# Feed-forward steps in another order: both score pairs around gate and up, the moments, then twelve down products, with a third bank for the scores

## The chip, the core and the metric

The kernel runs on one core of a Trainium2 chip. The metric is the device time of one execution in microseconds (us); the time before is the median of three runs. The engines are TensorE (PE in the profile, its weight loads PEld), VectorE (DVE), ScalarE (ACT), GpSimd (POOL) and SyncE (SP, which here only issues DMAs). They run their own instruction queues in order and meet at semaphores. TensorE writes to eight PSUM banks of 512 float32 columns.

## The reference

Eight batches of 256 rows by 512 columns go through two blocks:

```python
x = x + _L0_attn_ref(_L0_cond_ref(x, cond_2048[:, None, :], L0_cond_b), ...)   # causal conv, attention of 16 heads of 32
x = x + _L0_ffn_ref(_L0_cond2_ref(x, cond_2048, Wq, Wk, Wv, b), gate_cp, up_cp, down_cp)
...
gate = jnp.einsum('bsh,ih->bsi', hidden_states, gate_w)   # ih: 2048 x 512, from cubic splines of control points
up = jnp.einsum('bsh,ih->bsi', hidden_states, up_w)
inter = jax.nn.silu(gate) * up
return jnp.einsum('bsi,hi->bsh', inter, down_w)
```

The second attention (`cond2`) has 16 heads of 16 over 512 positions with a masked softmax; its result feeds the feed-forward network.

## The kernel before

The work is a software pipeline over batches. In the loop over batches 1 to 6 (and in batch 7 written out behind it) the second attention of batch b runs together with the feed-forward network of batch b - 1. Batch 0 has no feed-forward part, and the one of batch 7 runs alone at the end (the tail). GpSimd computes the convolution of batch b + 1 meanwhile: two operations, then seven pairs of a product (line 562) and an add (line 565), each on two SBUF operands, for every batch but the last.

**The window.** The change lies in the loop `for n in range(NT + 1)` of `batch` on TensorE, nine steps n = 0 to 8, each with the n-th 256 rows of the inner dimension 2048. In a step stand:
- `gate_up(b, n + 1)`, four products (eight records) on tiles of 64 rows, in banks 3 and 4. ScalarE takes the silu (line 604), VectorE multiplies (`gated`, line 780), ScalarE rounds the product to a high part (`inter_rounded`, line 611), and VectorE makes the low part (`rest`, line 785, two SBUF operands).
- `moments(b, n + 3)`, eight products (sixteen records) on tiles of 32 columns, from the attention result `y` and a table; ScalarE copies them to `z` (line 594), which gate and up of step n + 2 read.
- two pairs of `scores` from step 1 on (line 1131, 52 rows each, one of a pair on the upper and one on the lower half of the array), 32 in the window. Each is one bank; VectorE takes its row maximum (`maximum`, line 863).
- `down(b, n - 1, 1)` and `down(b, n, 0)`, six full-size products each (lines 995 to 997), into banks 6 and 7. The weights come in three slots by `load_weights` on SyncE, each when `down_step` says that a slot is free.

Step 5 (`TURN_STEP`) has `turn(0)`, a transpose of the first 16 maxima, from which `max_rows` makes rows for `shifted`. Steps 5 to 7 have no moments, steps 7 and 8 no gate and up; in step 8 `shifted(0)` and `shifted(1)` write banks 2 to 5.

**What sets the order.** Everything is written out by hand, on each engine, with counting semaphores. VectorE's loop over the same n has two maxima, `gated(n + 1)`, the turn in step 5, two maxima, `rest(n + 1)`. ScalarE's `feed` has per step `silu(n + 1)`, the copy of the moments, `inter_rounded(n + 1)`. The last one waits for TensorE as well, because `inter_h` has two slots; `down_step` counts the calls `down(b, m, 1)`:

```python
act.wait_ge(S["inter_out"], fed(b, "inter_out", n + 1))
if n >= 2:
    act.wait_ge(S["down_step"], fed(b, "down_step", n - 1))
nc.scalar.activation(r(inter_h[:, n % 2]), inter[:, n % 2], ACT.Copy).then_inc(S["inter_high"], 1)
```

A score waits until the maximum of the last score in its bank is taken: `wait("s2_max", last_in_bank + 1)`. The first score waits for `stack2_0` as well, twelve copies by SyncE (`stacks2(0)`, line 420) into `q2` and `k2`. Behind the window follow sixteen rounds with `shifted`, the other scores and `values2`.

Of the kernel before, what the change touches and what calls it, by code (L numbers as in the profile page):

```python
# [7 lines left out]
ACT = mybir.ActivationFunctionType  # L8
# [8 lines left out]
B, L, D = 8, 256, 512  # L17
# [14 lines left out]
NT = IT // 2  # L32
ZR = 32
# [29 lines left out]
WINDOW_SCORES = 4 * (NT + 1 - WINDOW_FROM)  # L63


AHEAD = 2
TURN_STEP = WINDOW_FROM + GS // 4
# [7 lines left out]
OUT_AT = tuple(CT * (g + 1) + (1 if CT * (g + 1) + 1 not in TURN_AT or g else 2) for g in range(NG - 1))  # L75


SCORE_BANKS = [s % 2 for s in range(WINDOW_SCORES)]
for _k in range(1, 1 + (NS - WINDOW_SCORES) // 4):
    for _s in range(4):  # L80
        _free = (0, 1) if _k in TURN_AT or _k in OUT_AT else (7, 0, 1)
        SCORE_BANKS.append(min(_free, key=lambda x: len(SCORE_BANKS) - 1 - SCORE_BANKS[::-1].index(x)
                               if x in SCORE_BANKS else -1))


FIRST_BANKS = [(0, 1, 3, 4)[s % 4] if s < WINDOW_SCORES - 4 else SCORE_BANKS[s] for s in range(NS)]
# [11 lines left out]
Q2_BANKS = (2, 5)  # L98
K2_BANKS = (6, 7)
V2_BANKS = (0, 1, 2, 5)  # L100
Z_BANKS = (2, 5)
GU_BANK, SUM_BANK = 3, 6
TURN_BANKS = (Z_BANKS[0], 7, 7, 7)

# [44 lines left out]
def fed(b, name, count):  # L149

    return b * PER_FEED[name] + (count - PER_FEED[name])


def block_program(nc, x_lanes, x_rows, taps, conv_b, qkv_wT, qk_b, v_b, out_wT, out_b, slopes, cond, w2T, att_b,
# [7 lines left out]
    with ExitStack() as ctx:  # L162
# [6 lines left out]
        psum = ctx.enter_context(nc.psum_tensor("psum", [P, 8, 512], F32))  # L169
# [51 lines left out]
        zt = sb("z_table", [P, CT, NT * 2 * ZR])  # L221
# [351 lines left out]
        def _(act):  # L573
# [16 lines left out]
            def z_copy(b, n):  # L590
                act.wait_ge(S["z_ready"], fed(b, "z_ready", n + 1))
                if n >= 2:
                    act.wait_ge(S["gu_ready"], fed(b, "gu_ready", n - 1))
                nc.scalar.activation(z[:, n % 2, :], psum[:, Z_BANKS[n % 2], 0:L], ACT.Copy).then_inc(S["z_out"], 1)

            def moments_out(b):
                for n in range(AHEAD):
# [138 lines left out]
        def _(dve):  # L736
# [64 lines left out]
            def batch(b, first=False, last=False):  # L801
# [88 lines left out]
                for n in range(NT + 1):  # L890
                    for s in window_pair(n, 0):
                        maximum(s)
                    if not first and n + 1 < NT:
                        gated(b, n + 1)
                    if n == TURN_STEP:
                        turn(0)
                    for s in window_pair(n, 1):
                        maximum(s)
                    if not first and n + 1 < NT:
                        rest(b, n + 1)  # L900
                if not first:
# [48 lines left out]
        def _(pe):  # L950
# [14 lines left out]

            def moments(b, n):
                if n >= 2:
                    pe.wait_ge(S["z_out"], fed(b, "z_out", n - 1))
                for i in range(2):
                    for s in range(4):  # L970
                        c = 2 * (s % 2) + i
                        cols = slice((2 * (n % NT) + s // 2) * ZR, (2 * (n % NT) + s // 2 + 1) * ZR)
                        last = nc.tensor.matmul(psum[s * ZR:(s + 1) * ZR, Z_BANKS[n % 2], 0:L], zt[:, c, cols],  # L973
                                                y[:, c, :], start=i == 0, stop=i == 1, skip_group_check=True)
                last.then_inc(S["z_ready"], 1)

# [59 lines left out]
            def batch(b, first=False, last_batch=False):  # L1036
                def wait(name, count):
                    pe.wait_ge(S[name], at(b, name, count))
# [74 lines left out]
                def scores(s):  # L1113
                    banks = FIRST_BANKS if first else SCORE_BANKS
                    last_in_bank = (FIRST_LAST_IN_BANK if first else LAST_IN_BANK)[s]
                    g, n = s // GS, s % GS
                    if n == 0:
                        wait(f"stack2_{g}", 192)
                        if g == 0:
                            wait("aug_rows", 64)  # L1120
                    if s < len(set(banks[:WINDOW_SCORES])):
                        wait("v2_out", CT)
                    elif last_in_bank is None:
                        wait("max2_low", 2)
                    else:
                        wait("s2_max", last_in_bank + 1)
                    if banks[s] == 7 and s >= WINDOW_SCORES + 4 * (OUT_AT[0] - 1):
                        wait("y_out", 1)
                    e, i, t = n % 2, n // (2 * CT), n // 2 % CT
                    rows = slice(e * ROWS2, e * ROWS2 + MAX2)  # L1130
                    nc.tensor.matmul(psum[:, banks[s], :], r(q2[rows, g, i, t * P:(t + 1) * P]),  # L1131
                                     r(k2[rows, g, i, :]), start=True, stop=True).then_inc(S["s2_ready"], 1)

                def turn(g):
                    wait("s2_max", GH * CT * (g + 1))
                    if g == 0 and first:
                        wait("v2_out", CT)
                    elif g == 0:
                        pe.wait_ge(S["z_out"], fed(b, "z_out", NT - 1))
                    elif g < NG - 1:  # L1140
                        wait("max2_low", g)
                        if g == 1 and first:
                            wait("k2_out", LT)
                        elif g == 1:
                            pe.wait_ge(S["sum_out"], fed(b, "sum_out", LT))
                    else:
                        wait("y_out", 1)
                    nc.tensor.transpose(psum[0:GH * CT, TURN_BANKS[g], 0:P], max2[:, g].rearrange("p e h t -> p (e h t)"), ident[:])\
                        .then_inc(S["max2_turned"], 1)

                def shifted(j):
                    g, u = j // (2 * CT), j % (2 * CT)
                    if u == 0:
                        wait("max2_rows", 64 * (g + 1))
                    if j < 2:
                        wait("v2_out", CT)
                        wait("k2_out", LT)
                        wait("max2_low", 1)
                        if first:
                            wait("s2_max", WINDOW_SCORES - 4)  # L1160
                        else:
                            pe.wait_ge(S["inter_out"], fed(b, "inter_out", NT))
                    else:
                        wait("p2_out", j - 1)
                    kt = u // 2
                    for e in range(2):
                        rows = slice(e * ROWS2, e * ROWS2 + END2)
                        last = nc.tensor.matmul(psum[:, 2 + u % 2 * 2 + e, :], r(k2[rows, g, u % 2, kt * P:(kt + 1) * P]),  # L1168
                                                r(q2[rows, g, u % 2, :]), start=True, stop=True)
                    last.then_inc(S["t2_ready"], 1)  # L1170
# [26 lines left out]
                    pe.wait_ge(fixed2, 64)  # L1197
                else:
                    wait("k2_out", LT)
                for n in range(NT + 1):  # L1200
                    if not first and n + 1 < NT:
                        gate_up(b, n + 1)
                    if not first and n == 0:
                        wait("v2_out", CT)
                        moments(b, AHEAD)
                    if not first and n + AHEAD + 1 < NT:
                        moments(b, n + AHEAD + 1)
                    for s in window_pair(n, 0):
                        scores(s)
                    if n == NT:  # L1210
                        shifted(0)
                    if n == TURN_STEP:
                        turn(0)
                    if not first and n:
                        down(b, n - 1, 1)
                    for s in window_pair(n, 1):
                        scores(s)
                    if n == NT:
                        shifted(1)
                    if not first and n < NT:  # L1220
                        down(b, n, 0)

                for k in range(1, ROUNDS + 1):
                    if k < ROUNDS:
# [226 lines left out]
```

## Time and profile before

| what | value |
|---|---|
| median of three runs | 1317.77 us |
| lowest and highest | 1312.59 and 1326.76 us |
| span of the profiled execution (no other time is recorded for it) | 1322.0 us |
| TensorE busy | 1216.3 us (92%) |
| VectorE busy | 780.9 us (59%) |
| ScalarE busy | 507.2 us (38%) |
| GpSimd busy | 355.0 us (27%) |
| maxima, line 863 | 512, 327.0 us busy |
| `rest`, line 785 | 64, 83.5 us busy, mean 1304 ns |

The busy shares are averages over the whole span. A window with its nine steps takes some 44 of the roughly 154 us of a batch. Where a line has the same operation at many places, the timeline of one stretch shows what it stands beside.

### The profile page before, as it was taken

What the parts mean: (1) busy time and instruction counts of PE and PEld (TensorE: products, weight loads), DVE (VectorE), ACT (ScalarE), POOL (GpSimd) and SP (SyncE); (2) the same over time, 40 slices, a digit from 0 to 9 for tenths busy, and PEclk for the clock granted to TensorE, in tenths of its full rate; (3) what the DMA queues carried; (4) which work ended last, traced back from release to release, by engine and by line L of the source; (5) the groups of instructions that cost most, each with busy time, mean ns of one, the idle gap of its engine ahead of it and who ended that gap; (6) DMA issues with size and microseconds to landing.
All of it is one profiled execution on the core that took longest, in us unless ns stands there. A gap on an engine that the chain in (4) does not pass through costs nothing.

```text
span 1322.0 us, 20809 instructions
## 1 busy us (share of the span) xinstructions
PE 1216.3 (92%) x7400; PEld 672.6 (51%) x7400; DVE 780.9 (59%) x1173; ACT 507.2 (38%) x699; POOL 355.0 (27%) x201
## 2 busy tenths in 40 slices
PE   5685789999999999999999999999999999999988
PEld 4352245554555545555546545555355555465436
DVE  7676644578445882568635783467725675356822
ACT  1131243334533265223633256322552336332572
POOL 3183770092003800075000910048000740000000
PEclk9687689998999999999999999999899989999999
DMA  8989604382226704265044822267042640448024
GB/s 294 279 318 309 175 2 112 139 193 103 49 67 173 238 23 112 98 154 182 14 102 146 208 80 66 53 178 229 23 112 108 167 159 15 100 149 221 36 113 175
DMA packets 81057, 180.89 MB, mean 137 GB/s; under 512 B 14468, under 2 KB 54356, under 8 KB 71284
## 3 DMA queue, kind: packets, MB, share of 16 engines
q1 hardware_dynamic: 70864, 161.56, 42.1%
q10 hardware_dynamic: 8832, 13.91, 3.1%
q0 software_dynamic: 1280, 4.20, 0.9%
q8 instruction: 68, 1.11, 0.4%
q14 instruction: 13, 0.11, 0.0%
HBM read 106.41 MB, written 21.14 MB: 96 GB/s over the span
## 4 chain that ended last, share of the span: by engine, by line
PE 75%; DVE 8%; DMA 6%; POOL 5%; issue 3%; ACT 2%; SPq 1%; ACTq 0%; DVEq 0%; POOLq 0%
PE psum L1181 9%; PE psum L1131 8%; PE psum L955 8%; PE psum L995 5%; PE psum L984 5%; PE psum L973 4%; PE psum L961 4%; DMA products<-in_gu_points 4%; DVE max L863 4%; PE psum L996 4%; PE psum L997 4%; PE psum L1089 4%; PE psum L1100 4%; PE psum L1168 3%; PE psum L1052 3%
## 5 line engine op out<-in xcount | busy, mean ns | idle before, releaser
L863 DVE TENSOR_REDUCE max<-psum 128x1 f32<-128x512 f32 x512 | 327.0, 684 | 111.3 <-PE psum L1131 109.4
L699 ACT ACTIVATE probs<-psum 128x1024 f32<-128x1024 f32 x256 | 248.0, 1022 | 168.2 <-PE psum L1168 166.9
L1131 PE MATMUL psum<-k,q 52*128 52x512 f32 x512 | 186.7, 514 | 28.8 <-DMA k<-low 15.2
L555 POOL TENSOR_TENSOR h<-h_in,tap 128x1024 f32<-128x1024 f32 x7 | 13.3, 1897 | 604.9 <-DVE low L766 604.9
L1131 PEld LDWEIGHTS psum<-k,q 52*128 52x128 f32 x512 | 79.3, 199 | 165.6 <-DVE max L863 129.5
L1181 PE MATMUL psum<-probs,v 128*32 128x512 f32 x1024 | 145.7, 643 | 0.4 <-ACT probs L699 0.3
L1168 PE MATMUL psum<-q,k 54*128 54x512 f32 x512 | 116.8, 452 | 14.7 <-DMA q<-max_l 7.2
L565 POOL TENSOR_TENSOR h<-h,products 128x1024 f32<-128x1024 f32 x49 | 123.5, 2520 | 3.8
L995 PE MATMUL psum<-stack 128*128 128x512 f32 x256 | 113.7, 444 | 0.0
L764 DVE CAST high<-low 128x1024 fp32r<-128x1024 f32 x32 | 25.3, 790 | 148.3 <-ACT low L586 120.6
L955 PE MATMUL psum<-h,qkv_w 128*128 128x256 f32 x448 | 105.9, 390 | 4.1 <-POOL h L565 4.1
L955 PEld LDWEIGHTS psum<-h,qkv_w 128*128 128x128 f32 x448 | 84.5, 194 | 32.7 <-issue 21.9
L996 PE MATMUL psum<-stack 128*128 128x512 f32 x256 | 100.9, 394 | 0.0
L997 PE MATMUL psum<-stack 128*128 128x512 f32 x256 | 100.3, 392 | 0.0
L785 DVE TENSOR_TENSOR stack<-probs,stack 128x512 fp32r<-128x512 f32 x64 | 83.5, 1304 | 26.7 <-ACT stack L611 26.7
L562 POOL TENSOR_TENSOR products<-h_in,tap 128x1024 f32<-128x1024 f32 x49 | 97.2, 1983 | 3.3
L653 ACT ACTIVATE probs<-psum 128x768 f32<-128x768 f32 x64 | 49.0, 810 | 92.9 <-PE psum L1072 92.9
L833 DVE RECIPROCAL inv<-psum 128x256 f32<-128x256 f32 x32 | 56.2, 1758 | 44.8 <-PE psum L1052 43.9
L611 ACT ACTIVATE stack<-probs 128x512 fp32r<-128x512 f32 x64 | 40.4, 631 | 109.5 <-DVE probs L780 102.5
L604 ACT ACTIVATE probs<-psum 128x512 f32<-128x512 f32 x64 | 38.2, 597 | 111.7 <-PE psum L984 111.7
L1168 PEld LDWEIGHTS psum<-q,k 54*128 54x128 f32 x512 | 55.3, 196 | 47.6 <-ACT probs L699 26.1
L961 PE MATMUL psum<-qkv_w,h 128*128 128x512 f32 x128 | 71.1, 677 | 2.7 <-issue 2.7
(112 smaller groups left out, 1645.7 us busy)
## 6 DMA issues: line engine op xcount, KB each, us to landing
stack<-wd_sorted SPq DMA_DIRECT2D x64, 1024.0 KB, 6.7
stack<-high SPq DMA_DIRECT2D x128, 128.0 KB, 2.4
stack<-low SPq DMA_DIRECT2D x64, 128.0 KB, 2.4
q<-high SPq DMA_DIRECT2D x128, 64.0 KB, 4.3
k<-high SPq DMA_DIRECT2D x128, 64.0 KB, 2.5
h_in<-in_x_lanes SPq DMA_DIRECT2D x9, 512.0 KB, 3.9
x<-in_x_rows SPq DMA_DIRECT2D x8, 512.0 KB, 7.9
x_scratch<-x SPq DMA_DIRECT2D x8, 512.0 KB, 3.9
```

Source lines behind the costliest of these rows:

```text
L562: nc.gpsimd.tensor_tensor(products[:], h_in[:, :, k:k + L], over(tap[:, :, k:k + 1]), ALU.mult)\
L565: nc.gpsimd.tensor_tensor(h[:], h[:], products[:], ALU.add).then_inc(S["conv_step"], 1)
L699: nc.scalar.activation(probs[:, u // 2 % 2, u % 2 * 2:u % 2 * 2 + 2, :], psum[:, 2 + u % 2 * 2:4 + u % 2 * 2, :], ACT.Exp)\
L863: nc.vector.reduce_max(max2[:, g, e, i, t:t + 1], psum[:, bank, :], AX_X).then_inc(S["s2_max"], 1)
L955: last = nc.tensor.matmul(psum[:, o % 2, 0:L], qkv_w[:, c, o * P:(o + 1) * P], h[:, c, :], start=c == 0, stop=c == CT - 1)
L961: last = nc.tensor.matmul(psum[:, V1_BANKS[t], :], h[:, c, t * P:(t + 1) * P], qkv_w[:, c, 2 * D:3 * D], start=c == 0, stop=c == CT - 1)
L995: nc.tensor.matmul(psum[:, SUM_BANK + s, :], r(inter_h[lhs]), r(w_h), start=n + g == 0, stop=False)
L996: nc.tensor.matmul(psum[:, SUM_BANK + s, :], r(inter_h[lhs]), r(w_l), start=False, stop=False)
L997: last = nc.tensor.matmul(psum[:, SUM_BANK + s, :], r(inter_l[lhs]), r(w_h), start=False, stop=n == NT - 1 and g == 1)
L1131: nc.tensor.matmul(psum[:, banks[s], :], r(q2[rows, g, i, t * P:(t + 1) * P]), r(k2[rows, g, i, :]), start=True, stop=True).then_inc(S["s2 ...
L1168: last = nc.tensor.matmul(psum[:, 2 + u % 2 * 2 + e, :], r(k2[rows, g, u % 2, kt * P:(kt + 1) * P]), r(q2[rows, g, u % 2, :]), start=True, ...
L1181: last = nc.tensor.matmul(psum[e * BLK:(e + 1) * BLK, 6, :], v2[:, t, head, :], probs[:, t % 2, e, :], start=t == 0, stop=t == CT - 1, ski ...
```

## The change

TensorE's step is written in another order: first score pair, gate and up, second score pair, in step 5 the turn, moments, `down(b, n - 1, 1)`, `down(b, n, 0)`. Step 8 stands behind the loop with its order as before. The scores of the window rotate over banks 0, 1 and 5 (the last four over 0 and 1) where they alternated between 0 and 1. Bank 5 is taken from the moments, which use bank 2 alone from the fifth on and so wait for the copy just before. VectorE takes the third maximum of a step ahead of `gated`, and the turn behind the fourth.

```diff
+def least_recent(banks, free):
+    return min(free, key=lambda x: len(banks) - 1 - banks[::-1].index(x) if x in banks else -1)
...
+    SCORE_BANKS.append(least_recent(SCORE_BANKS, (0, 1, 5) if _s < WINDOW_SCORES - 4 else (0, 1)))
...
-Z_BANKS = (2, 5)
+Z_BANKS = (2, 5, 2, 5, 2, 2, 2, 2)
...
                 for n in range(NT + 1):
                     for s in window_pair(n, 0):
                         maximum(s)
+                    for s in window_pair(n, 1)[:1]:
+                        maximum(s)
                     if not first and n + 1 < NT:
                         gated(b, n + 1)
+                    for s in window_pair(n, 1)[1:]:
+                        maximum(s)
                     if n == TURN_STEP:
                         turn(0)
-                    for s in window_pair(n, 1):
-                        maximum(s)
                     if not first and n + 1 < NT:
                         rest(b, n + 1)
...
-                    pe.wait_ge(S["z_out"], fed(b, "z_out", n - 1))
+                    pe.wait_ge(S["z_out"], fed(b, "z_out", n - 1 if n <= 2 * AHEAD else n))
...
+                        if banks[s] == Z_BANKS[1] and not first:
+                            pe.wait_ge(S["z_out"], fed(b, "z_out", 2 * AHEAD))
...
-                        if first:
-                            wait("s2_max", WINDOW_SCORES - 4)
-                        else:
+                        wait("s2_max", WINDOW_SCORES - 4)
+                        if not first:
                             pe.wait_ge(S["inter_out"], fed(b, "inter_out", NT))
...
-                for n in range(NT + 1):
+                for n in range(NT):
+                    for s in window_pair(n, 0):
+                        scores(s)
                     if not first and n + 1 < NT:
                         gate_up(b, n + 1)
+                    for s in window_pair(n, 1):
+                        scores(s)
+                    if n == TURN_STEP:
+                        turn(0)
...
                     if not first and n + AHEAD + 1 < NT:
                         moments(b, n + AHEAD + 1)
-                    for s in window_pair(n, 0):
-                        scores(s)
-                    if n == NT:
-                        shifted(0)
-                    if n == TURN_STEP:
-                        turn(0)
                     if not first and n:
                         down(b, n - 1, 1)
-                    for s in window_pair(n, 1):
-                        scores(s)
-                    if n == NT:
-                        shifted(1)
-                    if not first and n < NT:
+                    if not first:
                         down(b, n, 0)
```

TensorE, step 1 of a batch's window, before (line 984 gate and up, 973 moments, 1131 scores, 995 to 997 down):

```order
L984 MATMUL psum<-z,w_gate_up 128x256 x4
L973 MATMUL psum<-y,z_table 32x256 x8
L1038 ISA x2
L1131 MATMUL psum<-k,q 128x512 x2
L995 MATMUL psum<-stack 128x512
L996 MATMUL psum<-stack 128x512
```

The same place in the changed kernel (991 gate and up, 980 moments, 1140 scores, 1002 to 1004 down):

```order
L1140 MATMUL psum<-k,q 128x512 x2
L985 REGISTER_ALU
L991 MATMUL psum<-z,w_gate_up 128x256 x4
L1131 REGISTER_ALU
L1140 MATMUL psum<-k,q 128x512
L1045 REGISTER_ALU
L1140 MATMUL psum<-k,q 128x512
L980 MATMUL psum<-y,z_table 32x256 x8
L1002 MATMUL psum<-stack 128x512
L1003 MATMUL psum<-stack 128x512
```

All four scores stand ahead of the moments now, and all twelve down products behind them.

VectorE, one step of the window, before (863 maxima, 780 `gated`, 785 `rest`; in the changed kernel 868, 785 and 790):

```order
L863 TENSOR_REDUCE max<-psum 128x1
L803 REGISTER_ALU
L863 TENSOR_REDUCE max<-psum 128x1
L779 REGISTER_ALU
L780 TENSOR_TENSOR probs<-psum,probs 128x512
L803 REGISTER_ALU
L863 TENSOR_REDUCE max<-psum 128x1
L803 REGISTER_ALU
L863 TENSOR_REDUCE max<-psum 128x1
L785 TENSOR_TENSOR stack<-probs,stack 128x512
```

and in the changed kernel:

```order
L790 TENSOR_TENSOR stack<-probs,stack 128x512
L808 ISA
L868 TENSOR_REDUCE max<-psum 128x1
L808 REGISTER_ALU
L868 TENSOR_REDUCE max<-psum 128x1
L808 REGISTER_ALU
L868 TENSOR_REDUCE max<-psum 128x1
L784 REGISTER_ALU
L785 TENSOR_TENSOR probs<-psum,probs 128x512
L808 REGISTER_ALU
L868 TENSOR_REDUCE max<-psum 128x1
L790 TENSOR_TENSOR stack<-probs,stack 128x512
```

The third maximum has moved ahead of `gated`; `rest` is still the last of the step, and ahead of the next step's first maximum.

## Rows read from the trace of the kernel before

**Rows 1.** The page: the chain of waits that ended last, by engine.

```profile
PE 75%; DVE 8%; DMA 6%; POOL 5%; issue 3%; ACT 2%; SPq 1%; ACTq 0%; DVEq 0%; POOLq 0%
```

**Rows 2.** Stretches of core 0: us, busy time by engine, PEclk, DMA share, GB/s.

```profile
575.60:581.72 6.12, 6.12 (x41) 3.58 (x41) 4.53 (x7) 1.62 (x3) 5.88 (x4) 1.00 0.61 100
...
600.06:604.97 4.91, 4.91 (x26) 3.18 (x25) 3.91 (x9) 1.23 (x2) 4.75 (x3) 1.00 1.04 223
604.97:610.96 5.99, 5.46 (x25) 3.35 (x25) 5.99 (x8) 1.93 (x3) 2.19 (x1) 1.00 0.98 398
610.96:614.97 4.01, 4.01 (x17) 2.47 (x16) 2.91 (x5) 0.79 (x2) 2.37 (x2) 1.00 0.05 19
```

**Rows 3.** The timeline of TensorE, step 2: start us, us, engine, line, operation.

```profile
581.72 1.14 PE L984 MATMUL psum<-z,w_gate_up 64*128 64x256 f32 x8
...
582.78 1.07 PE L973 MATMUL psum<-y,z_table 128*32 128x256 f32 x16
...
583.78 0.50 PE L1131 MATMUL psum<-k,q 52*128 52x512 f32 x2
...
584.22 0.53 PE L995 MATMUL psum<-stack 128*128 128x512 f32 x1
...
585.28 0.40 PE L996 MATMUL psum<-stack 128*128 128x512 f32 x1
...
585.52 0.39 PE L997 MATMUL psum<-stack 128*128 128x512 f32 x1
...
585.84 0.50 PE L1131 MATMUL psum<-k,q 52*128 52x512 f32 x2
```

**Rows 4.** The timeline of VectorE and ScalarE in the same step.

```profile
584.32 1.29 DVE L863 TENSOR_REDUCE max<-psum 128x1 f32<-128x512 f32 x2 [0.32 <-PE psum L1131]
...
586.32 0.63 ACT L611 ACTIVATE stack<-probs 128x512 fp32r<-128x512 f32 x1 [2.02 <-DVE probs L780]
...
587.58 1.21 DVE L785 TENSOR_TENSOR stack<-probs,stack 128x512 fp32r<-128x512 f32 x1
```

**Rows 5.** The timeline of GpSimd, 569 to 616 us.

```profile
581.09 2.37 POOL L565 TENSOR_TENSOR h<-h,products 128x1024 f32<-128x1024 f32 x1
...
585.85 2.39 POOL L565 TENSOR_TENSOR h<-h,products 128x1024 f32<-128x1024 f32 x1
...
588.31 2.23 POOL L562 TENSOR_TENSOR products<-h_in,tap 128x1024 f32<-128x1024 f32 x1
...
593.09 1.90 POOL L562 TENSOR_TENSOR products<-h_in,tap 128x1024 f32<-128x1024 f32 x1
...
604.78 2.38 POOL L565 TENSOR_TENSOR h<-h,products 128x1024 f32<-128x1024 f32 x1
```

**Rows 6.** The timeline of TensorE, step 5.

```profile
600.06 1.14 PE L984 MATMUL psum<-z,w_gate_up 64*128 64x256 f32 x8
...
601.36 0.28 PE L1148 MATMUL psum<-ident,max 128*16 128x128 f32 x1
```

**Rows 7.** The timeline of VectorE and TensorE, step 6; PEld is the weight load.

```profile
604.96 2.74 DVE L785 TENSOR_TENSOR stack<-probs,stack 128x512 fp32r<-128x512 f32 x1
...
608.36 0.18 PEld L1131 LDWEIGHTS psum<-k,q 52*128 52x128 f32 x1 [0.86 <-DVE max L863]
...
608.96 0.18 PEld L1131 LDWEIGHTS psum<-k,q 52*128 52x128 f32 x1 [0.41 <-DVE max L863]
...
609.38 0.50 PE L995 MATMUL psum<-stack 128*128 128x512 f32 x1
```

**Rows 8.** SyncE's copies into `k2` before step 1, and line 420's landing, 574.5 to 575.2.

```profile
574.17 1.23 SPq L420 DMA_DIRECT2D k<-low  x2
...
DMA to landing us min/median/max: 2.3/2.3/2.3
```

**Rows 9.** The timeline of TensorE, batch 7, scores of steps 1 and 8.

```profile
1192.78 0.50 PE L1131 MATMUL psum<-k,q 52*128 52x512 f32 x2 [0.42 <-DMA k<-low]
...
1229.00 0.50 PE L1131 MATMUL psum<-k,q 52*128 52x512 f32 x2
```

More of the change, by code:

```diff
@@ L75 @@
 OUT_AT = tuple(CT * (g + 1) + (1 if CT * (g + 1) + 1 not in TURN_AT or g else 2) for g in range(NG - 1))
-SCORE_BANKS = [s % 2 for s in range(WINDOW_SCORES)]
+def least_recent(banks, free):
+    return min(free, key=lambda x: len(banks) - 1 - banks[::-1].index(x) if x in banks else -1)
+SCORE_BANKS = []
+for _s in range(WINDOW_SCORES):
+    SCORE_BANKS.append(least_recent(SCORE_BANKS, (0, 1, 5) if _s < WINDOW_SCORES - 4 else (0, 1)))
 for _k in range(1, 1 + (NS - WINDOW_SCORES) // 4):
@@ L81 @@
         _free = (0, 1) if _k in TURN_AT or _k in OUT_AT else (7, 0, 1)
-        SCORE_BANKS.append(min(_free, key=lambda x: len(SCORE_BANKS) - 1 - SCORE_BANKS[::-1].index(x)
-                               if x in SCORE_BANKS else -1))
+        SCORE_BANKS.append(least_recent(SCORE_BANKS, _free))
 FIRST_BANKS = [(0, 1, 3, 4)[s % 4] if s < WINDOW_SCORES - 4 else SCORE_BANKS[s] for s in range(NS)]
@@ L593, in z_copy @@
                     act.wait_ge(S["gu_ready"], fed(b, "gu_ready", n - 1))
-                nc.scalar.activation(z[:, n % 2, :], psum[:, Z_BANKS[n % 2], 0:L], ACT.Copy).then_inc(S["z_out"], 1)
+                nc.scalar.activation(z[:, n % 2, :], psum[:, Z_BANKS[n % NT], 0:L], ACT.Copy).then_inc(S["z_out"], 1)
             def moments_out(b):
@@ L972, in moments @@
                         cols = slice((2 * (n % NT) + s // 2) * ZR, (2 * (n % NT) + s // 2 + 1) * ZR)
-                        last = nc.tensor.matmul(psum[s * ZR:(s + 1) * ZR, Z_BANKS[n % 2], 0:L], zt[:, c, cols],
+                        last = nc.tensor.matmul(psum[s * ZR:(s + 1) * ZR, Z_BANKS[n % NT], 0:L], zt[:, c, cols],
                                                 y[:, c, :], start=i == 0, stop=i == 1, skip_group_check=True)
@@ L1138, in turn @@
                     elif g == 0:
-                        pe.wait_ge(S["z_out"], fed(b, "z_out", NT - 1))
+                        pe.wait_ge(S["z_out"], fed(b, "z_out", NT))
                     elif g < NG - 1:
@@ L1207, in batch @@
                         moments(b, n + AHEAD + 1)
-                    for s in window_pair(n, 0):
-                        scores(s)
-                    if n == NT:
-                        shifted(0)
-                    if n == TURN_STEP:
-                        turn(0)
                     if not first and n:
                         down(b, n - 1, 1)
-                    for s in window_pair(n, 1):
-                        scores(s)
-                    if n == NT:
-                        shifted(1)
-                    if not first and n < NT:
-                        down(b, n, 0)
+                    if not first:
+                        down(b, n, 0)
+                for s in window_pair(NT, 0):
+                    scores(s)
+                shifted(0)
+                if not first:
+                    down(b, NT - 1, 1)
+                for s in window_pair(NT, 1):
+                    scores(s)
+                shifted(1)
                 for k in range(1, ROUNDS + 1):
```

## The prediction

> **What bounds the kernel now.** First the chain of waits [rows 1]: three quarters of the span lie on TensorE and 8% on VectorE, so the order of TensorE's queue is what counts. Then the table of stretches [rows 2], cut at the steps of one batch's feed-forward window (batch 3; batches 1 to 6 repeat it to within some hundredths). TensorE is busy through every full step, at full clock; step 1 takes 6.12 us, and steps 2 to 4 take 6.11. GpSimd is busy through nearly all of it too, with the convolution of the next batch. Steps 5, 6 and 7 take 4.91, 5.99 and 4.01 us. From step 1 to the start of step 8 the window takes 614.97 - 575.60 = 39.37 us. Last, the timeline inside one step [rows 3, 4] and at the two places where an engine waits [rows 7, 8]. Below, SC is a pair of scores, GU gate and up, MO the moments, DN one call of down (six products).
>
> **What TensorE saves.** In [rows 3] GU to MO is 1.06 us, MO to SC 1.00, SC to DN 0.44, DN to the next SC 585.84 - 584.22 = 1.62. Two more pieces (SC 0.42, DN 1.57 before the next GU) make up the 6.11. A DN takes six products at about 0.23 (585.28 to 585.52) and the rest of its 1.62 is entry and exit: each change of kind costs some 0.2. In step 5, without MO, GU and SC stand next to each other and take 601.36 - 600.06 = 1.30 [rows 6], against 1.06 + 0.44 = 1.50 apart: both use half-height tiles, and no change is paid. New step: SC, GU, SC is 1.30 plus one pair more at 0.21 (512 columns, half of 0.42 less the entry) = 1.51; MO 1.00; twelve products 1.62 + 6 x 0.23 = 3.00. Sum 5.51, so **0.60 us saved** in a full step if nothing waits. The Trainium skill (TensorEngine Tiling (Array Packing), Key Properties) says that a change of tiling mode, not of tile, drains TensorE; the trace agrees, with its 1.30 against 1.50. By that rule alone, at equal price, six changes become three; it has no price.
>
> **New wait 1: copies of the stack.** SC now opens step 1. Its operands come last with two copies that SyncE issues from 574.17 to 575.40, the second at about 574.8, landing 2.3 later [rows 8]: 577.15, where TensorE is ready at 575.60. Today GU and MO (2.06 us) cover this; afterwards they stand behind the wait. Cost 1.55 us a batch. In batch 7 even today SC waits, until 1192.78 [rows 9].
>
> **New wait 2: the last score of a step.** With three banks the fourth score of a step (4k+3) needs the maximum of the first (4k) of the same step. The first maximum starts 0.54 after SC (583.78 to 584.32), takes 0.68 (two take 1.29) [rows 3, 4] and the weight load follows at 0.05: 1.27 after the start of the step, then 0.42 to the next kind (608.96 to 609.38) [rows 7]. So MO starts 1.69 into the step instead of 1.51, and a full step is 1.69 + 1.00 + 3.00 = 5.69. Still 0.42 better than now.
>
> **New wait 3, which decides: the rounding.** ScalarE's `inter_rounded(n + 1)` waits for `down_step` of down(n - 1, 1), whose operand it overwrites. Today that DN ends at 585.91, before the gated product is there, and costs nothing. Now it stands behind both score pairs and the moments. From the start of MO: 1.00 to DN, 1.69 to the end of its sixth product (584.22 to 585.52 + 0.39), rounding 0.63 [rows 4], and 0.05 and 0.04 for the hand-overs to ScalarE and VectorE: VectorE's `rest` can start 3.41 us after MO. VectorE works in order, so behind `rest` is queued the first maximum of the next step, for that maximum waits the fourth score, and behind that score TensorE holds MO and twelve products. That closes a loop: end of `rest` to the fourth score's load 0.66 (604.96 + 2.74 = 607.70 to 608.36), 0.42 to MO, 3.41 to `rest`: **4.49 us** plus the duration of `rest`.
>
> And `rest` is not 0.68 us long here. In [rows 4, 5] the one at 587.58 lasts 1.21 and ends 0.55 after GpSimd's add ends (585.85 + 2.39 = 588.24); the one at 604.96 lasts 2.74 and ends 0.54 after the add of 604.78 ends [rows 5, 7]. So `rest` waits for the GpSimd instruction that it meets, and runs then. The Trainium skill (SBUF — State Buffer, SBUF: two separate sides) calls this an exclusive lock, held for a whole instruction by whichever starts first, between GpSimd and a VectorE operation with two SBUF inputs. The trace agrees; by that rule with a full 0.68 behind the lock every meeting would end 0.13 later than by the rows, and the sum would stay.
>
> Now the steps of batch 3 by hand. If a GpSimd operation ends at e, `rest` ends at e + 0.55; the third GpSimd operation from there starts at e + 4.85 (583.46 to 588.31 [rows 5]); the next `rest` arrives at e + 0.55 + 4.49 = e + 5.04. It falls **0.2 us after that third operation began** and sits it out (1.90 or 2.38 long [rows 5]).
> Step 1: SC 577.15, MO 578.84, DN 579.84; `rest` 582.25 falls in the add of 581.09 to 583.46, ends 584.01. Step 2 starts at 582.84.
> Step 2: fourth score 584.67, MO 585.09, DN 586.09; `rest` 588.50 meets the operation from 588.31 to 590.21, ends 590.76. Step 3 at 589.09.
> Step 3: MO 591.84, DN 592.84; `rest` 595.25 meets the add of 595.06 to 597.44, ends 597.99. Step 4 at 595.84.
> Step 4: MO 599.07, DN 600.07; `rest` 602.48 meets the operation from 602.29 to 604.19, ends 604.74. Step 5 at 603.07, against 600.06 now.
> Step 5: fourth score 605.40, turn and DN 605.85; step 6 at 608.85. Here GpSimd's last add ends near 607.0 and `rest` (608.3) is free. Steps 6 and 7 have no MO: 1.27 + 0.42 + 3.00 = 4.69 each; the fourth score of step 7 waits likewise. Step 8 at **618.2 against 614.97: 3.2 us later**. Today's stall in step 6 (5.99 against 4.91) goes, and the loop of steps 2 to 4 takes more. The rounds behind start from the scores and `shifted` of step 8, and nothing in them gives time back. Six batches: +19.3.
>
> Batch 7 has no convolution, so `rest` takes 0.68 and TensorE sets the pace: from 1192.78 four steps of 5.69, one of 4.72, two of 4.69 = 36.86, against 1229.00 - 1192.78 = 36.22 now [rows 9]: +0.6.
>
> **What costs nothing.** Moments all in bank 2 from the fifth on: their copy is 0.4 us and has most of a step. The later turn: SyncE is still issuing copies. In batch 0, which has no feed-forward part, the turn comes two maxima (1.2 us) later, once, behind SyncE's copies. The extra wait of `shifted(0)` for 28 maxima is met in step 7. Batch B's tail keeps its order; the earlier copy it now waits for is a step old. The load of the last weight block starts after down(4, 1), some 4 us later than now, and is needed as much later. An uncovered one would cost up to 1 us a batch.
>
> **Sum**: 19.3 + 0.6 = 19.9, say +19 us. The profiled execution spans 1322.0 us, 4 above the median of the three runs and inside their range; the difference is laid on the median: 1317.8 + 19 = **1337 us**.
>
> **Rivals.**
> (a) The loop is a little shorter than 4.49. Below 4.29, `rest` of step 2 arrives before 588.31 and ends at 588.79. Worked on the same way, steps start at 588.9, 594.5, 600.6, 606.8, 611.6 and 616.2 (the next ones meet GpSimd again): +1.3 a batch, +8: 1326. For it: the margin of 0.2 in a sum of nine pieces. Against: the two longest pieces are single rows.
> (b) Not slower: `rest` meets GpSimd no more than today and TensorE sets the pace. +1.55 for the stack, 4 x (5.69 - 6.11), then 14.10 against 14.91 for steps 5 to 7: -0.9 a batch, -5: 1313. It decides if the rounding comes more than about 1 us sooner than I have it, so that `rest` slips in ahead. The rows on which MO and DN rest speak against it.
> (c) The first copies land before step 1 and no fourth score waits: then 0.60 in four steps and more in the last three, some 3 to 4 us a batch: 1293. Copies and their landing [rows 8] are against it. The lists of instructions show that the order is indeed changed, so that "nothing changes" is no case.
> (d) Worse: a weight load or a DMA late on top, +1 a batch: 1344.
>
> **Chances.** Forecast 0.55, (a) 0.18, (b) 0.15, (c) 0.04, (d) 0.08. A measurement of this kernel tells about 1% (13 us) from no change, the three runs being 14 apart. Forecast and (d) are over that, less a tenth for noise: slower 0.57; (a) and (b) and the rest within: 0.37; faster 0.06. The range takes in (a), the forecast and most of (b): 1312 to 1344.
>
> **What the profile after will show.** Right: SC of step 1 held some 1.5 us by the copies; steps 2 to 4 of batches 1 to 6 at 6.2 to 7.2 us, with the fourth score's load waiting for VectorE, `rest` near 2 to 2.5 us long and ScalarE's rounding released by down; in batch 7 steps of 5.7. Wrong: a `rest` of 0.7 in most steps, rounding released by VectorE, or no wait at step 1.

## The result and the profile after

The changed kernel takes 1343.6 us in the median of four runs (1340.5 to 1345.0), the kernel before 1316.5 in the median of four. The ratio is 1.017, with an interval from 1.013 to 1.021: slower, by a little more or a little less than 2%. (The ratio of these two medians is 1.021. Timed again, in 13 runs, the kernel before takes 1320.6 us in the median, and beside that the changed one is at 1.017.) The two profiled executions span 1341.6 and 1322.0 us, 19.6 apart.

The page of the changed kernel, its span, its engines and its chain of waits:

```profile
span 1341.6 us, 20811 instructions
...
PE 1203.4 (90%) x7400; PEld 682.4 (51%) x7400; DVE 786.9 (59%) x1173; ACT 507.3 (38%) x699; POOL 356.8 (27%) x201
...
PE 67%; DVE 10%; issue 7%; DMA 6%; POOL 4%; SPq 3%; ACT 3%; ACTq 0%; DVEq 0%; POOLq 0%
```

TensorE is busy for 13 us less than before (1216.3), which fits a step with three changes of tile mode in place of six. Its share of the chain falls from 75% [rows 1] to 67%, and VectorE's rises from 8% to 10%. The largest rise, "issue" from 3% to 7%, is time for which the profile shows no wait, so the chain alone does not say where the time went.

Steps 1 to 7 of batch 3 in the table of stretches (us, busy time of TensorE, weight loads, VectorE, ScalarE and GpSimd, clock, DMA share, GB/s), each from its first score to that of the next:

```profile
583.10:588.73 5.63, 5.62 (x40) 3.93 (x40) 3.66 (x6) 1.61 (x3) 5.47 (x3) 1.00 0.64 105
588.73:594.83 6.10, 5.96 (x41) 3.82 (x40) 4.65 (x7) 1.62 (x3) 5.87 (x4) 1.00 0.87 241
594.83:601.60 6.77, 5.97 (x41) 3.83 (x40) 5.31 (x7) 1.61 (x3) 6.53 (x4) 1.00 0.90 234
601.60:608.81 7.21, 5.96 (x42) 3.83 (x41) 5.76 (x7) 1.62 (x3) 6.97 (x4) 1.00 0.84 242
608.80:614.57 5.77, 4.97 (x27) 3.43 (x26) 5.74 (x9) 1.23 (x2) 3.90 (x2) 1.00 0.66 204
614.57:619.30 4.73, 4.73 (x27) 3.48 (x26) 3.86 (x7) 1.92 (x3) 0.00 (x0) 1.00 0.94 364
619.30:623.90 4.60, 4.05 (x17) 2.59 (x16) 2.50 (x5) 0.80 (x2) 4.30 (x3) 1.00 0.06 19
```

[rows 2] are the same steps before. Step 1 is fast at 5.63; from there each step is longer than the last, until GpSimd has ended its convolution in step 5. The timeline of VectorE, ScalarE, GpSimd and TensorE through step 3 shows why:

```profile
593.58 0.63 ACT L616 ACTIVATE stack<-probs 128x512 fp32r<-128x512 f32 x1 [1.17 <-PE psum L1004]
594.12 1.90 POOL L567 TENSOR_TENSOR products<-h_in,tap 128x1024 f32<-128x1024 f32 x1
594.25 2.32 DVE L790 TENSOR_TENSOR stack<-probs,stack 128x512 fp32r<-128x512 f32 x1 [1.45 <-ACT stack L616]
...
596.49 1.27 DVE L868 TENSOR_REDUCE max<-psum 128x1 f32<-128x512 f32 x2
597.22 0.18 PEld L1140 LDWEIGHTS psum<-k,q 52*128 52x128 f32 x1 [1.21 <-DVE max L868]
...
600.35 0.63 ACT L616 ACTIVATE stack<-probs 128x512 fp32r<-128x512 f32 x1 [1.18 <-PE psum L1004]
...
600.86 2.36 POOL L570 TENSOR_TENSOR h<-h,products 128x1024 f32<-128x1024 f32 x1
601.02 2.76 DVE L790 TENSOR_TENSOR stack<-probs,stack 128x512 fp32r<-128x512 f32 x1 [1.46 <-ACT stack L616]
```

Read it as a loop. The rounding (L616) is released by down (L1004), where before VectorE's product released it [rows 4]. `rest` (L790) arrives at 594.25, 0.13 us after a GpSimd operation began at 594.12, and ends 0.55 after that one ends (596.02). The maximum behind it releases the fourth score at 597.22, and the moments and six down products behind that score release the next rounding at 600.35. Again `rest` comes 0.16 us too late, at 601.02 against 600.86. All of batches 1 to 6 repeat this: in steps 2, 3 and 4 `rest` comes 0.13 to 0.16 us after a GpSimd operation began. Over the whole run the same shows in the groups of waits:

```profile
DVE stack L790 <- ACT stack L616: 72.3, 57, 3.1
...
ACT stack L616 <- PE psum L1004: 67.0, 48, 2.5
```

The second group stood at 7.0 us, six times, in the trace of the kernel before.

**A yardstick for what follows.** The part ahead of batch 1 differs by up to 13 us from one profile to the next, whatever the kernel (step 0 of batch 1 starts between 259.1 and 271.7 us; without e3, the latest, between 259.1 and 265.4), and single spans with it. So the window itself is compared: from the start of step 0's gate and up to `shifted(0)`. Before, it takes 44.2 us in batches 1 to 6 and 43.6 in batch 7; in the changed kernel 47.3 to 47.4 and 45.1. That is 6 x 3.13 + 1.5 = 20.3 us in all, against 19.6 in the spans.

### The profile page after: what moved, and what is told of

The parts are those of the page before. It is cut to its first block, busy times and chain, and to the rows that moved or that the text cites. A ratio compares the mean times of both kernels' runs of the same rounds, so it can differ in the third digit from the quotient of the medians.

```text
span 1341.6 us, 20811 instructions
## 1 busy us (share of the span) xinstructions
PE 1203.4 (90%) x7400; PEld 682.4 (51%) x7400; DVE 786.9 (59%) x1173; ACT 507.3 (38%) x699; POOL 356.8 (27%) x201
## 4 chain that ended last, share of the span: by engine, by line
PE 67%; DVE 10%; issue 7%; DMA 6%; POOL 4%; SPq 3%; ACT 3%; ACTq 0%; DVEq 0%; POOLq 0%
PE psum L1189 9%; PE psum L1140 8%; PE psum L962 8%; PE psum L1002 4%; DVE max L868 4%; PE psum L980 4%; PE psum L1096 4%; PE psum L1004 3%; PE psum L1003 3%; PE psum L968 3%; PE psum L1059 3%; DMA products<-in_gu_points 3%; PE psum L1107 3%; PE psum L1176 3%; PE psum L1076 3%
## 5 line engine op out<-in xcount | busy, mean ns | idle before, releaser
L1140 PE MATMUL psum<-k,q 52*128 52x512 f32 x512 | 202.3, 514 | 59.6 <-DVE max L868 27.6
L1140 PEld LDWEIGHTS psum<-k,q 52*128 52x128 f32 x512 | 86.4, 198 | 195.1 <-DVE max L868 133.7
L790 DVE TENSOR_TENSOR stack<-probs,stack 128x512 fp32r<-128x512 f32 x64 | 87.7, 1370 | 72.3 <-ACT stack L616 72.3
L1002 PE MATMUL psum<-stack 128*128 128x512 f32 x256 | 108.0, 422 | 0.0
L1003 PE MATMUL psum<-stack 128*128 128x512 f32 x256 | 100.6, 393 | 0.0
L1004 PE MATMUL psum<-stack 128*128 128x512 f32 x256 | 100.3, 392 | 0.0
L838 DVE RECIPROCAL inv<-psum 128x256 f32<-128x256 f32 x32 | 56.2, 1758 | 48.1 <-PE psum L1059 47.3
L658 ACT ACTIVATE probs<-psum 128x768 f32<-128x768 f32 x64 | 49.1, 810 | 92.8 <-PE psum L1079 92.8
L616 ACT ACTIVATE stack<-probs 128x512 fp32r<-128x512 f32 x64 | 40.4, 632 | 82.9 <-PE psum L1004 67.0
L815 DVE TENSOR_REDUCE max<-psum 128x2 f32<-128x256 f32 (+1 forms) x128 | 63.0, 551 | 13.8 <-PE psum L1030 12.2
```

What stands on the lines that cost most here:

```text
L790: nc.vector.tensor_tensor(r(inter_l[:, n % 2]), inter[:, n % 2], inter_h[:, n % 2], ALU.subtract)\
L1002: nc.tensor.matmul(psum[:, SUM_BANK + s, :], r(inter_h[lhs]), r(w_h), start=n + g == 0, stop=False)
L1003: nc.tensor.matmul(psum[:, SUM_BANK + s, :], r(inter_h[lhs]), r(w_l), start=False, stop=False)
L1004: last = nc.tensor.matmul(psum[:, SUM_BANK + s, :], r(inter_l[lhs]), r(w_h), start=False, stop=n == NT - 1 and g == 1)
```

## The experiments

Steps here run from gate and up to gate and up. Window times are of single profiles; where a median is given the kernel was timed too.

| kernel | window, batches 1 to 6 | batch 7 | median us | ratio to before |
|---|---|---|---|---|
| before | 44.2 | 43.6 | 1316.5 | |
| changed | 47.3 to 47.4 | 45.1 | 1343.6 | 1.017 |
| e1 `rest` behind the maximum | 43.6 to 46.8 | 45.7 | 1317.8 | 0.998 [0.995, 1.001] |
| e2 down ahead of the moments | 47.3 (batch 1: 49.8) | 44.0 | 1344.4 | 1.020 [1.016, 1.024] |
| e3 changed, convolution cut | 43.2 to 44.3 | 45.5 | one run | |
| e4 before, convolution cut | 43.2 to 43.3 | 43.5 | one run | |
| e5 as e2, rounding first | 45.4 (batches 1, 2: 45.8, 48.5) | 44.3 | one run | |
| e6 gate and up open step 1 | 47.3 | 42.6 | 1339.7 | 1.016 [1.011, 1.021] |
| e7 e6 with e1 | 43.7 to 45.0 | 44.8 | 1317.2 | 0.998 [0.995, 1.000] |
| e8 changed, two banks | 49.1 to 50.7 (batch 1: 52.9) | 49.0 | one run | |
| e9 e1 with the old step 1 | 41.9 to 43.6 | 43.2 | 1318.0 | 0.996 [0.994, 0.999] |

e1, e2, e6 and e7 were timed beside a kernel before at 1320.6 in the median, e9 beside one at 1323.3.

**e1: take the maximum out from behind `rest`.** VectorE's loop:

```diff
-                    for s in window_pair(n, 0):
+                    for s in window_pair(n, 0)[:1]:
+                        maximum(s)
+                    if not first and 1 < n < NT:
+                        rest(b, n)
+                    for s in window_pair(n, 0)[1:]:
                         maximum(s)
...
-                    if not first and n + 1 < NT:
+                    if not first and n == 0:
                         rest(b, n + 1)
```

> The changed kernel with one move on VectorE: the low part of step n (rest) stands behind the first maximum of step n instead of ahead of it. Loop theory (down holds the rounding, rest meets GpSimd, the first maximum queues behind rest, the fourth score waits for it): the loop is cut, steps 2 to 5 fall from 6.1, 6.8, 7.2 and 5.8 us to 5.65 and 4.7, some 4.2 us less in batches 1 to 6; about 1317 us, level with the kernel before. Rival, the copies that hold step 1: they are untouched, so 1338 to 1342. Rival, the fourth score's wait for the first maximum as such: also untouched, no change.

Measured: 1317.8 us, ratio to the kernel before 0.998; two per cent of the run came back by the place of one instruction. Steps 2 to 4 take 5.65 to 5.69 us in all seven batches. In batches 1, 4 and 7, with windows of 45.5, 46.8 and 45.7, step 1 is 7.24, 7.13 and 6.95 us long instead of 5.65, because TensorE runs at half clock in it, behind its wait for the copies. Added up, the seven windows are 14.5 us shorter than in the changed kernel, and the medians are 26 us apart; the profile does not show all of the gain. The table of stretches for steps 2 and 3, and the timeline of step 4, batch 3:

```profile
580.73:586.38 5.65, 5.65 (x43) 3.82 (x41) 4.81 (x6) 1.61 (x3) 5.41 (x4) 1.00 0.86 263
586.38:592.03 5.65, 5.65 (x42) 3.84 (x40) 3.94 (x6) 1.62 (x3) 5.49 (x3) 1.00 0.64 144
```

```profile
592.42 2.37 POOL L570 TENSOR_TENSOR h<-h,products 128x1024 f32<-128x1024 f32 x1
592.68 0.47 PEld L1144 LDWEIGHTS psum<-k,q 52*128 52x128 f32 x2
592.83 2.50 DVE L790 TENSOR_TENSOR stack<-probs,stack 128x512 fp32r<-128x512 f32 x1
```

TensorE is busy for all of the 5.65. `rest` still meets GpSimd and lasts 2.50 us, and it costs nothing there: the fourth score's weights (592.68) are loaded while it waits. So neither `rest` nor GpSimd is the cost by itself; it is the maximum queued behind them. Steps 6 and 7 together take 0.4 to 1.9 us more than their 9.3 in the changed kernel: in batches 3, 4 and 5 the moved `rest(7)` meets GpSimd's addition of the output bias.

**e2 and e5: release the rounding sooner.** e2 moves `down(b, n - 1, 1)` ahead of the moments on TensorE:

```diff
+                    if not first and n:
+                        down(b, n - 1, 1)
                     if not first and n == 0:
                         wait("v2_out", CT)
                         moments(b, AHEAD)
                     if not first and n + AHEAD + 1 < NT:
                         moments(b, n + AHEAD + 1)
-                    if not first and n:
-                        down(b, n - 1, 1)
```

> The changed kernel with down(n - 1, 1) put between the second score pair and the moments, so that slot 2 of the rounded product is free 1 us sooner, at the price of one more change of tile mode (0.2 us). Loop theory: rest arrives 1 us sooner, about 4.0 us behind the end of the GpSimd operation it sat out, inside the second operation from there and not the third; steps 2 to 4 near 5.9 us, 2 to 3 us a batch less than the changed kernel: 1322 to 1330 us. Rival, the copies or the third bank: no gain, 0.2 us a step more, about 1345 us.

Measured: 1344.4 us, window 47.3 in batches 2 to 6, steps 6.1, 6.7 and 7.2 as without the edit. The expectation was wrong, and the rival had named this time. The timeline of ScalarE and VectorE in e2:

```profile
596.12 0.38 ACT L599 ACTIVATE z<-psum 128x256 f32<-128x256 f32 x1 [3.28 <-PE psum L980]
596.40 0.62 ACT L616 ACTIVATE stack<-probs 128x512 fp32r<-128x512 f32 x1
597.06 2.47 DVE L790 TENSOR_TENSOR stack<-probs,stack 128x512 fp32r<-128x512 f32 x1 [1.75 <-ACT stack L616]
```

The rounding follows the copy of the moments without a gap, and that copy waited 3.28 us for TensorE's moments, which now stand behind down. The rounding is held by its own queue. From the fourth score to `rest` it is now 4.09 us (592.97 to 597.06), where the changed kernel has 3.80 (597.22 to 601.02). So e2 did not shorten the loop and cannot tell it from its rivals. It shows something else: `rest` comes 0.3 us later, 0.46 us after a GpSimd operation began (596.60), and the window stays the same. e5 mends this in `feed`, with the TensorE edit kept:

```diff
+                    if n:
+                        inter_rounded(b, n + 1)
                     for m in range(AHEAD if n == 0 else n + AHEAD + 1, min(n + AHEAD + 2, NT)):
                         z_copy(b, m)
-                    inter_rounded(b, n + 1)
+                    if n == 0:
+                        inter_rounded(b, n + 1)
```

> The kernel with down(n - 1, 1) ahead of the moments, and ScalarE's rounding now ahead of the copy of the moments. Why the former run kept steps of 6.1, 6.7 and 7.2 us: there the rounding no longer waited for down but for the moments' copy, which stands ahead of it in ScalarE's queue and had moved behind down. Loop theory: with both out of the way the loop is 1.4 us shorter, rest arrives inside the second GpSimd operation from the one it sat out, and the steps come near TensorE's own 5.9 us; window from step 0 to shifted(0) 44.3 to 45.5 us instead of 47.3. Rival, that the loop is not the cause: 47.3 as before.

Measured: window 45.4 us in batches 3 to 6, as expected; steps 3 and 4 take 5.9, step 2 6.0 to 6.1. Steps 6 and 7 together take 10.5 us where the changed kernel has 9.3. Batch 2 has 48.5, all of the excess in steps 6 and 7: there the `rest` at 456.62 meets GpSimd's addition of the output bias (456.38 to 458.75) and lasts 2.69 us, the last score behind it waits, and from 461.6 to 465.0 TensorE runs at half clock. The wait of that score, batch 2:

```profile
459.96 0.50 PE L1143 MATMUL psum<-k,q 52*128 52x512 f32 x1 [2.03 <-DVE max L871]
```

The timeline of e5 in a full step, batch 3:

```profile
597.30 0.63 ACT L616 ACTIVATE stack<-probs 128x512 fp32r<-128x512 f32 x1 [1.39 <-PE psum L1007]
597.71 1.90 POOL L567 TENSOR_TENSOR products<-h_in,tap 128x1024 f32<-128x1024 f32 x1
597.97 2.19 DVE L793 TENSOR_TENSOR stack<-probs,stack 128x512 fp32r<-128x512 f32 x1 [0.45 <-ACT stack L616]
...
600.33 1.89 DVE L871 TENSOR_REDUCE max<-psum 128x1 f32<-128x512 f32 x3 [0.17 <-PE psum L1143]
```

`rest` is 2.19 us long and yet VectorE is back at the maxima before their scores (0.17 us idle): with the loop shorter than TensorE's step, the meeting is covered.

**e3 and e4: no GpSimd to meet.** In both kernels the sixteen operations of the convolution work on 8 columns instead of 1024, of which this is one:

```diff
-                    nc.gpsimd.tensor_tensor(h[:], h[:], products[:], ALU.add).then_inc(S["conv_step"], 1)
+                    nc.gpsimd.tensor_tensor(h[:, 0:1, 0:8], h[:, 0:1, 0:8], products[:, 0:1, 0:8], ALU.add).then_inc(S["conv_step"], 1)
```

> The changed kernel with the convolution's sixteen GpSimd operations in the loop cut to 8 of 1024 columns (the rest of h keeps old values, so the output is not the reference's). Loop theory: rest takes 0.69 us everywhere, all full steps take 5.65 us as in batch 7, and the window from step 0 to shifted(0) takes 43.1 us instead of 47.3. Rival, the copies alone: the window stays 1.6 us a batch above that of the kernel before with the same cut.

> The kernel before with the same cut of the convolution (the output is not the reference's). Loop theory: full steps keep 6.11 us, step 6 loses its stall, and the window takes 43.2 us instead of 44.2; so this kernel and the changed one with the same cut stand within 3 us of each other in the span, where they are 20 apart with the convolution. Rival, copies or banks: they stay 10 to 20 apart.

Measured: in the window both parts came out, the first nearly. The changed kernel's steps 2 to 4 take 5.65 to 5.69 us in batches 1 to 6, and its windows 43.2 to 44.3 (mean 43.7) where 43.1 was expected, the kernel before 43.2. So of 3.1 us between the two 0.5 is left without GpSimd. Part of this is a late weight load: in batches 2, 4 and 6 of e3 TensorE waits 0.84, 0.25 and 0.71 us for `stack<-wd_sorted` in step 6. The changed kernel has no such wait. The spans are 1323.8 and 1308.9, 15 apart, which by itself would fit the rival; but 12.6 of the 15 lie ahead of step 0 of batch 1 (271.71 against 259.07), where the change only moves the turn of batch 0 by two maxima. Behind it they are 2.3 apart. The bound of 3 us on spans was set without knowing how that part scatters.

**e6 and e7: cover the copies again.** e6 lets gate and up and the moments open step 1, and leaves the rest:

```diff
                 for n in range(NT):
+                    if not first and n == WINDOW_FROM:
+                        gate_up(b, n + 1)
+                        moments(b, n + AHEAD + 1)
                     for s in window_pair(n, 0):
                         scores(s)
-                    if not first and n + 1 < NT:
+                    if not first and n + 1 < NT and n != WINDOW_FROM:
                         gate_up(b, n + 1)
...
-                    if not first and n + AHEAD + 1 < NT:
+                    if not first and n + AHEAD + 1 < NT and n != WINDOW_FROM:
                         moments(b, n + AHEAD + 1)
```

> The changed kernel with one edit: in step 1 alone gate and up and the moments stand ahead of the four scores, so that the last copies of the stack are covered again. Loop theory: rest of step 1 falls into the same GpSimd add as in the changed kernel and ends at the same time, so from there nothing is gained in batches 1 to 6: window 47.0 to 47.4 us still, though TensorE's wait of 1.6 us in step 1 is gone. Batch 7 gains some 1.5 us, and the half clock behind its wait, another 1.5. Median 1337 to 1341. Rival, the copies as the cause: 1.6 us less in every batch, window 45.7, median 1330.

Measured: window 47.3 us in all of batches 1 to 6, with TensorE's wait for the copies gone there. Steps 0 to 4 take 4.5, 7.0, 6.75, 6.75 and 7.2 us against 6.5, 5.65, 6.1, 6.8 and 7.2. Steps 0 and 1 together are thus only 0.6 us shorter (11.55 against 12.19), not 1.6. The rest is lost to the edit itself: with four scores in a row the fourth waits for the first maximum with nothing to cover it, and step 1 takes 7.05 in batch 7 too, where GpSimd does nothing. That wait, batch 7:

```profile
1207.74 0.73 PE L1140 MATMUL psum<-k,q 52*128 52x512 f32 x3
1209.02 0.50 PE L1140 MATMUL psum<-k,q 52*128 52x512 f32 x1 [0.55 <-DVE max L868]
```

The 0.6 us that remain are lost in step 2, and to GpSimd. The timeline of e6 in step 1, batch 3:

```profile
583.74 2.38 POOL L570 TENSOR_TENSOR h<-h,products 128x1024 f32<-128x1024 f32 x1
584.38 2.29 DVE L790 TENSOR_TENSOR stack<-probs,stack 128x512 fp32r<-128x512 f32 x1 [0.43 <-ACT stack L616]
584.96 0.50 PE L1140 MATMUL psum<-k,q 52*128 52x512 f32 x2
```

`rest` comes 0.64 us after the add began, where it comes 1.29 after it in the changed kernel, and waits for the same end, 12.9 us after the start of the window in both. From there the pace is GpSimd's. What the copies cost in batches 1 to 6 is not shown by this. Without the whole 1.64 us of waiting, the changed kernel's `rest` of step 1 (588.15) would come at 586.51, ahead of the start of that add (586.86), into the operation before it; no run has this. Batch 7, without GpSimd and now without half clock, gains 2.5 us.

> Both edits: gate and up and moments open step 1, and rest stands behind the first maximum of the next step. Loop theory: TensorE paces every step, no wait in step 1 and no half clock behind one: window 42.9 to 44 us in all batches against 44.2 of the kernel before, median 1306 to 1313. Rival, that the two costs are one and the same: nothing over the run with rest moved alone (1318).

Measured: 1317.2 us, ratio 0.998. The expectation was too good by 4 us at least. Steps 2 to 4 are at 5.65, but putting all four scores together in step 1 keeps it at 7.0, and steps 5 to 7 lose 1.3 to 2.5 us where the moved `rest` meets GpSimd. In batch 7 the copies were late all the same (0.69 us of waiting), TensorE fell to half clock, and step 1 took 9.4 us.

**e8: is the third bank the harm?** The edit is `(0, 1)` for `(0, 1, 5)` in the window's rotation.

> The changed kernel with the window's scores on banks 0 and 1 alone. The fourth score then waits for the second maximum of its step, 0.6 us later than for the first. Loop theory: rest still falls into the third GpSimd operation, so steps 2 to 4 keep 6.1 to 7.2 us and the delay shows once there and again in steps 5 to 7: window 48.5 to 50 us. Rival, that three banks are the harm: window at or under 47.3.

Measured: 49.1 us in batches 2 and 5 and 50.7 in the others but the first, the steps of batch 7 6.25 instead of 5.65. The third bank is worth 0.6 us a full step in this order, and is not the harm. Steps 2 and 3 are 6.25 and 6.6 us, no longer than in the changed kernel: the meetings with GpSimd fell differently. In batches 3, 4 and 6, which lie above the expected 48.5 to 50, TensorE runs at half clock in step 7 (in batch 3 from 630.4 to 633.8), and steps 6 and 7 together take 12.1 us instead of 10.5.

**e9: the best of both.** As e1, with step 1 alone in the order of the kernel before:

```diff
                 for n in range(NT):
+                    if not first and n == WINDOW_FROM:
+                        gate_up(b, n + 1)
+                        moments(b, n + AHEAD + 1)
+                        for s in window_pair(n, 0):
+                            scores(s)
+                        down(b, n - 1, 1)
+                        for s in window_pair(n, 1):
+                            scores(s)
+                        down(b, n, 0)
+                        continue
```

> Rest behind the first maximum, and step 1 alone in the order of the kernel before (gate and up, moments, pair, down, pair, down); steps 2 to 7 in the changed order. Against the run in which gate and up and moments merely open step 1: no wait for the first maximum in step 1, 6.3 us there instead of 7.0, and no half clock in step 1 of batch 7 (9.4 us there). Loop theory and the account of the two costs: some 7 us less than that run's 1317, near 1310; window 43.0 to 44.3 us. Rival, that what is left lies in GpSimd's meetings with the moved rest in steps 6 and 7 and shifts with the start: no gain over 1317.

Measured: windows of 41.9 to 43.6 us and 43.2 in batch 7, shorter than before in every batch; ratio to the kernel before 0.996, interval 0.994 to 0.999. The median of 1318.0 is not the 1310 expected, beside a kernel before at 1323.3. So the new order, with `rest` moved and the old step 1, is worth some 5 us. How much of this the moved `rest` would give the kernel before by itself, which stalls in step 6 [rows 7], no run tells. The profiled run spans 1307.1, but a single profile is no measure of that. Something else is late now. In step 6 of batches 1, 3, 6 and 7 TensorE waits 0.7 to 1.4 us for the weights of down; in batch 3:

```profile
599.46 0.50 PE L1006 MATMUL psum<-stack 128*128 128x512 f32 x1 [1.15 <-DMA stack<-wd_sorted]
```

The shorter window no longer covers a load of weights, a cost that the prediction had priced at up to 1 us a batch for the last block.

## Why the prediction was right

The forecast was 1337 us, slower by the loop; measured were 1343.6, with 19.6 us between the spans where the sum had 19.9. The mechanism was right. That the spans agree to 0.3 us is in part luck: the part ahead of batch 1 moves single spans by several us, and two errors offset each other, 0.1 us a batch too much in batches 1 to 6 (3.2 for 3.13) and 0.9 us too little in batch 7.

- **What TensorE saves.** Right. A full step at TensorE's own pace was put at 5.69 with the fourth score's wait; measured 5.63 and 5.65. Half-height tiles next to each other pay no change [rows 6], and TensorE's busy time fell by 13 us.
- **New wait 3.** Right in mechanism, place and size. By hand the steps from 1 on came to 5.69, 6.25, 6.75, 7.23, 5.78 and 4.69 us; measured in batch 3: 5.63, 6.10, 6.77, 7.21, 5.77, 4.73. `rest` was to fall 0.2 us after a GpSimd operation began; it does by 0.13 and 0.16. e1 and e3 each break the loop at another of its links, e5 shortens it, and each time the long steps go. e2 adds that ScalarE's order is a link as well, which I had passed over: the copy of the moments stands ahead of the rounding.
- **New wait 1.** Its size was right (1.55 expected, 1.64 measured) and its place in the account wrong. I wrote it as a cost of 1.55 us a batch. In the loop a wait does not pass through one to one. e6 makes the first `rest` 0.65 us earlier and batches 1 to 6 gain nothing, since it falls into the same add. This does not make the cost nothing: by the prediction's own times a `rest` 1.55 us earlier, at 580.70 instead of 582.25, would miss the add of 581.09 and end a whole operation sooner. With the loop cut, the old step 1 is worth 1.2 to 1.3 us in steps 0 and 1 (e9 has 10.96 us there, e1 12.16 to 12.27 where it keeps its clock). What the copies cost in the changed kernel stays open.
- **New wait 2.** The 0.18 us of the fourth score is in the steps of 5.65. e8 shows what two banks would have done, 0.6 us a full step more.
- **Batch 7.** Expected +0.6, measured +1.5 (45.13 against 43.63). Step 1 took 7.24 us instead of 5.69. The table of stretches gives the reason, in its clock column (the value ahead of the last two):

```profile
1209.00:1211.60 2.60, 0.56 (x3) 0.14 (x1) 0.68 (x1) 0.00 (x0) 0.00 (x0) 1.00 0.63 103
1211.60:1213.30 1.70, 1.68 (x12) 1.23 (x12) 1.15 (x2) 0.27 (x1) 0.00 (x0) 1.00 0.69 109
1213.30:1215.20 1.90, 1.90 (x18) 0.61 (x17) 1.90 (x4) 0.33 (x1) 0.00 (x0) 0.50 0.61 101
1215.20:1216.60 1.40, 1.40 (x7) 1.15 (x4) 0.03 (x1) 0.38 (x1) 0.00 (x0) 0.50 0.59 100
```

  TensorE stood idle for 2.05 us before the first score, and from 1213.3 it ran at 1.2 instead of 2.4 GHz for 3.3 us. The copies I had reckoned with; that half clock can follow a wait, and cost 1.6 us here, I had not.
- **Rivals.** (a), the loop short enough to slip ahead of GpSimd, was the nearest: it missed by 0.13 us. (b) and (c) did not occur; a state much like (b) is what e1 makes. (d), 1344 us by something late on top, has the measured median, and is not what happened: TensorE waits for no weights in any window of the changed kernel, and the windows grew by 3.13 us each, not by 4.2. The 7 us between forecast and median lie in where the sum was laid: on the median of three runs, 1317.8, though the profile that it was worked out from spans 1322.0; that span and 19.9 make 1341.9, and 1341.6 was measured. The median is 27 us higher than that of its partner's four runs and 23 above the 1320.6 of the later ones; the interval (17 to 28 us) holds these and the 19.6.

What stays open: why batch 0 and the part ahead of it scatter by 13 us, what the copies cost in batches 1 to 6, and what the moved `rest` would do in the old order.

## What to carry to other kernels

When instructions of one kind are packed together on the bounding engine, ask of every other engine what its in-order queue now waits for behind that pack, and follow the waits round until they close. If the loop is longer than the step, a saving on the bounding engine is lost; find the one instruction that can move out from behind the wait, as the maximum here. The two-operand SBUF instruction on VectorE, 0.69 us by itself, ended 0.55 us behind the GpSimd instruction that it met and so took up to 2.8 us, so put such an instruction where nothing urgent is queued behind it.

## What the runs showed of the hardware that was not expected

- Once `rest` waits for GpSimd, the two can lock in step: in batches 1 to 6 `rest` comes 0.13 to 0.16 us after a GpSimd operation has begun in steps 2 to 4, each time at the cost of a whole operation (1.9 or 2.4 us). The windows of the six batches differ by less than 0.1 us, and neither a first `rest` 0.65 us earlier (e6) nor a loop 0.3 us longer (e2, batches 2 to 6) moved them.
- An idle time of 2.05 us on TensorE ahead of the first score was followed by 3.3 us at half clock in batch 7; one of 1.64 us in batch 3 was not. In e1 idle times of 1.90 and 1.87 us (batches 1 and 4) were followed by half clock, and step 1 took 7.24 and 7.13 us instead of 5.65. But in batch 1 of the changed kernel 1.92 us, and in that of e3 1.91, were not, and step 1 kept its 5.65 and 5.68. So near 1.9 us the length of the wait alone does not decide.
